# A mixture-of-experts block on one core: token rows scattered to memory in slot order, and blocks turned by VectorE

## What is computed

```python
h = _rmsnorm(x, pre_norm_w)                       # here x is xn
a = sigmoid(h @ w_a + decay_bias); i_gate = sigmoid(h @ w_i); v = h @ w_v
rec_out = _chunked_scan(a, sqrt(clip(1 - a*a, 1e-8)) * (i_gate * v))
x = x + rec_out @ out_proj_w
h2 = _rmsnorm(x, ffn_norm_w)
gate, up = split(h2 @ w_gate_up, 2)               # 256 -> 2 x 1024
branch_1 = x + silu(gate) * up @ w_down           # 1024 -> 256
...
top_vals, top_idx = top_k(xn @ w_router, 2)       # 8 experts, two per token
probs = softmax(top_vals)
branch_2 = sum over the two experts e of  probs_e * (square(relu(xn @ w_fc[e])) @ w_proj[e])
```

## Time and profile before

| | |
|---|---|
| median of 3 runs | 288.37 us (287.87 to 289.13) |
| the profiled execution's own time | 287.88 us |
| its span, first to last instruction | 286.1 us |

### The profile page before, as it was taken

One profiled execution on the slowest core, in us unless ns is written; L12 is line 12 of the kernel. 1 busy time (PEld: TensorE's weight loads), 2 busy tenths in 40 slices (PEclk: granted clock), 3 DMA queues, 4 the chain that ended last, 5 costly groups with the idle time before them and its releaser, 6 DMA issues.

```text
span 286.1 us, 5565 instructions
## 1 busy us (share of the span) xinstructions
PE 277.3 (97%) x1781; PEld 244.2 (85%) x1781; DVE 202.6 (71%) x467; ACT 171.2 (60%) x366; POOL 145.9 (51%) x139
## 2 busy tenths in 40 slices
PE   5989999999999999999999999999999999999995
PEld 5867778789889888898999789989999999887895
DVE  3899999999988888745557786545456544446973
ACT  3798889989669455536675554546568454532331
POOL 6498020433840136774878776666777775620000
PEclk9999999999999999999999999999999999999999
DMA  6999990018993002344345444434444445449922
GB/s 204 358 375 383 385 410 2 0 14 143 259 268 68 19 25 47 65 74 56 60 74 78 74 58 74 75 57 58 76 77 72 81 68 64 51 97 354 307 75 76
DMA packets 32584, 36.92 MB, mean 129 GB/s; under 512 B 4390, under 2 KB 29740, under 8 KB 32524
## 3 DMA queue, kind: packets, MB, share of 16 engines
q0 software_dynamic: 9616, 13.01, 28.4%
q1 hardware_dynamic: 20672, 21.31, 22.6%
q10 hardware_dynamic: 2268, 2.23, 2.2%
HBM read 24.68 MB, written 13.96 MB: 135 GB/s over the span
## 4 chain that ended last, share of the span: by engine, by line
PE 77%; DMA 9%; DVE 5%; issue 3%; POOL 3%; ACT 1%; POOLq 0%; SPq 0%; DVEq 0%; ACTq 0%
PE ps L401 63%; DMA acc_dram<-yb,gather_u 7%; PE ps L489 5%; PE ps L667 5%; DMA sums<-acc_dram 2%; PE ps L405 1%; PE ps L502 1%; PE ps L418 1%; DVE hT_lo L1103 1%; POOL rn L1522 1%; DVE Wpj_lo L1264 1%; DVE guT_lo L1274 0%; DVE stats L1075 0%; DVE X L1306 0%; DVE dec L1134 0%
## 5 line engine op out<-in xcount | busy, mean ns | idle before, releaser
L1570 POOL DMA_INDIRECT xg<-xh_dram,gather_u x39 | 46.5, 1192 | 47.3 <-DVE picks L1331 34.0
L1579 POOL DMA_INDIRECT acc_dram<-yb,gather_u x39 | 62.0, 1591 | 16.3 <-issue 9.2
L401 PE MATMUL ps<-h2T_lo,Wgu_hi 128*128 128x512 f32 (+1 forms) x132 | 42.9, 386 | 0.0
L401 PE MATMUL ps<-h2T_hi,Wgu_hi 128*128 128x512 f32 (+1 forms) x132 | 40.9, 391 | 0.0
L401 PE MATMUL ps<-h2T_hi,Wgu_lo 128*128 128x512 f32 (+1 forms) x132 | 40.1, 385 | 0.0
L401 PE MATMUL ps<-Wd_hi,guT_hi 128*128 128x256 f32 x128 | 36.3, 284 | 0.6 <-DVE guT_lo L1274 0.5
L1348 DVE TENSOR_TENSOR aT_lo<-ps,aT_hi 128x256 fp32r<-128x256 f32 x39 | 16.5, 424 | 28.1 <-ACT aT_hi L926 27.7
L401 PE MATMUL ps<-Wd_hi,guT_lo 128*128 128x256 f32 x128 | 36.2, 282 | 0.0
L401 PE MATMUL ps<-Wd_lo,guT_hi 128*128 128x256 f32 x128 | 36.1, 282 | 0.0
L884 ACT ACTIVATE gu<-ps 128x512 f32<-128x512 f32 x31 | 18.4, 595 | 20.4 <-PE ps L401 20.4
L1269 DVE TENSOR_TENSOR gu<-gu,ps 128x512 f32<-128x512 f32 x31 | 21.2, 684 | 13.0 <-PE ps L401 11.6
(11 more groups left out here) (194 smaller groups left out, 665.6 us busy)
## 6 DMA issues: line engine op xcount, KB each, us to landing
sums<-acc_dram SPq DMA_DIRECT2D x8, 512.0 KB, 7.5
acc_dram<-zero SPq DMA_DIRECT2D x1, 2176.0 KB, 14.6
Wgu_raw<-in_L_attn_w_gate_up_dram SPq DMA_DIRECT2D x4, 512.0 KB, 9.1
Wfc_raw<-in_L_ffn_w_fc_dram SPq DMA_DIRECT2D x4, 512.0 KB, 13.9
xh_dram<-X ACTq DMA_DIRECT2D x4, 512.0 KB, 7.7
Wpj_raw<-in_L_ffn_w_proj_dram SPq DMA_DIRECT2D x4, 512.0 KB, 9.8
X<-in_L_attn_x_dram SPq DMA_DIRECT2D x3, 512.0 KB, 6.7
out_dram<-X SPq DMA_DIRECT2D x3, 512.0 KB, 4.8
```

Source lines behind the costliest of these rows:

```text
L401: return nc.tensor.matmul(dst, lhs, rhs, start=start, stop=stop, skip_group_check=group)
L1570: pool.indirect_dma_start(out=xg[i % XG][:, :], out_offset=None, in_=xh_dram, in_offset=bass.IndirectOffsetOnAxis(ap=gather_u[:, i:i + 1], ...
L1579: pool.indirect_dma_start(out=acc_dram[i % 2], in_=yb[i % YB][:, :], in_offset=None, compute_op=ALU.add, out_offset=bass.IndirectOffsetOnA ...
```

## The change

The inversion of the slot list goes. Instead each token row, with its weight and its home (the row to which its output goes) in two more columns, is scattered by GpSimd to a DRAM array `xs_dram` in slot order: 32 indirect stores of 128 rows (16 groups of tokens, two experts each). The array is first filled with blank rows. SP then loads pairs of blocks from it, each in eight transfers of 32 columns on 32 partitions, so that 32x32 squares lie together; VectorE transposes the squares (`block_turn`), one block ahead, and TensorE no longer turns blocks. The weights and homes of all slots are loaded once (`of_slot`). An expert's output row is written, without addition, to its own row of `y_dram`, one of two for each token; SP loads both sets as the two sums. x itself is added to the residual by an accumulating transfer of GpSimd's (`add_x`). Weight pieces 6 to 10 are halved by ScalarE and VectorE, as the others, instead of by accumulating transfers. The blocks move from slices 8 to 23 to slices 9 to 24. The rows of x lie 258 instead of 256 numbers apart in SBUF.

The diff, cut to its core:

```diff
-        FIRST = 8
-        LAST = 23
-        THREE = (14, 19, 23)
+        FIRST = 9
+        LAST = 24
+        THREE = (14, 19, 24)
...
@@ the list of SP @@
+            sp.dma_start(xs_slot[:, :, 0:D], blank[:, None, :].to_broadcast([P, 2 * NP, D])).then_inc(blank_stored, 16)
+            sp.dma_start(xs_slot[:, :, D:ROW].bitcast(I32), no_home[:, :, :]).then_inc(blank_stored, 16)
...
-            sp.wait_ge(routed, 1)
             sp.wait_ge(experts_ready, 1)
             for n in range(UNDER_ROUTING, ALL):
                 load_piece(n)
+            for b in range(B):
+                sp.wait_ge(rows_stored[b], 16 * TOP * J)
+            for n in range(NP):
+                if n >= XQ:
+                    sp.wait_ge(turned, 2 * (n - XQ) + 2)
+                for r in range(P // Q):
+                    mine = xq[n % XQ][r * Q:(r + 1) * Q].rearrange("i v g k c -> i (v g) k c")
+                    for k in range(K):
+                        col = k * P + r * Q
+                        sp.dma_start(mine[:, :, k, :], xs_pair[n, :, :, col:col + Q]).then_inc(xq_loaded[n % XQ], 16)
+                if n == 0:
+                    sp.dma_start(of_slot[:, :, :], xs_slot[:, :, WEIGHT:ROW]).then_inc(of_slot_loaded, 16)
             sp.wait_ge(fc_done, NB)
...
@@ the list of PE @@
-                if d == SLOTS:
-                    slots()
...
             def expert_in(i):
-                if i < NB:
-                    pe.wait_ge(xg_loaded[i % XG], 16 * (i // XG + 1))
...
-                    block_transpose(T1, xg[i % XG], t1_done)
...
@@ the list of DVE @@
             def add_residual(b, side):
                 dve.wait_ge(q_ready, 1)
-                dve.wait_ge(xh_stored[b], 16)
+                if b:
+                    dve.wait_ge(rows_stored[b], 16 * TOP * J)
...
+            def block_turn(i):
+                if i < NB:
+                    dve.wait_ge(xq_loaded[i // 2 % XQ], 16 * K * (P // Q) * (i // 2 // XQ + 1))
+                    if i >= 2:
+                        dve.wait_ge(xg_hi, i - 1)
+                    V.transpose(xr[i % 2][:, :, :].rearrange("p k (g s) -> p k g s", s=Q),
+                                xq[i // 2 % XQ][:, i % 2, :, :, :].rearrange("p g k c -> p k g c")).then_inc(turned, 1)
...
             gated_value(2, 1)
-            blocks(0)
-            blocks(1)
             weights_lo(5)
             gated_value(3, 0)
-            lanes(0)
-            lanes(1)
+            gated_value(3, 1)
             up(0)
-            lanes(2)
-            gated_value(3, 1)
+            cumulate(1, 0)
             split_gu(0)
             up(1)
-            lanes(3)
+            recur(1, 0)
             split_gu(1)
...
+            weights_lo(9)
+            weights_lo(10)
+            up(6)
             weights_lo(11)
-            up(6)
+            split_gu(6)
+            split_h2(1)
             weights_lo(12)
-            split_gu(6)
+            up(7)
             weights_lo(13)
-            split_h2(1)
-            up(7)
+            split_gu(7)
             weights_lo(14)
+            up(8)
+            take_down(0, 0)
+            block_turn(0)
+            block_in(0)
             for d in range(FIRST, B * M):
                 if d <= LAST:
                     for v, i in enumerate(blocks_of(d)):
-                        block_in(i)
+                        block_turn(i + 1)
...
                         block_square(i)
-                        block_weight(i)
+                        block_in(i + 1)
                         if i == 0:
                             weights_lo(16)
...
@@ the list of POOL @@
+            def mark_rows(k, first, end):
+                if k == 0:
+                    pool.wait_ge(prob_ready, TOP)
+                else:
+                    for b in range(first, end):
+                        pool.wait_ge(rows_stored[b], 16 * J)
+                n = end - first
+                mine = slice(J * first, J * end)
+                for b in range(first, end):
+                    G.iota(home_col[:, b, :], pattern=[[P, J]], base=k * N + b * J * P, channel_multiplier=1)
+                chain.step(G.tensor_tensor(weight_col[:, first:end, :],
+                                           prob[:, k, mine].rearrange("p (b j) -> p b j", j=J),
+                                           q2[:, mine].rearrange("p (b j) -> p b j", j=J), ALU.mult))
+            def store_rows(k, b):
+                if k == 0 and b == 0:
+                    pool.wait_ge(slots_ready, 1)
+                    pool.wait_ge(blank_stored, 32)
+                for j in range(J):
+                    n = k * T + b * J + j
+                    pool.indirect_dma_start(out=xs_dram, in_=rows_x[:, b, j, :], in_offset=None,
+                                            out_offset=bass.IndirectOffsetOnAxis(ap=slot_u[:, n:n + 1], axis=0)
+                                            ).then_inc(rows_stored[b], 16)
+            def add_x(b):
+                pool.wait_ge(h2_ready, b + 1)
+                pool.dma_start(Y[b][:, :, :], x_t[b], accum_op=ALU.add).then_inc(x_added[b], 16)
...
             def scatter(i):
                 pool.wait_ge(y_ready, i + 1)
-                if i >= 2:
-                    pool.wait_ge(*added(i - 2))
-                pool.indirect_dma_start(out=acc_dram[i % 2], in_=yb[i % YB][:, :], in_offset=None, compute_op=ALU.add,
-                                        out_offset=bass.IndirectOffsetOnAxis(ap=gather_u[:, i:i + 1], axis=0)
-                                        ).then_inc(y_added[i % 2], 16)
+                if i == 0:
+                    pool.wait_ge(of_slot_loaded, 16)
+                pool.indirect_dma_start(out=y_dram, in_=yb[i % YB][:, :], in_offset=None,
+                                        out_offset=bass.IndirectOffsetOnAxis(ap=of_slot[:, i, 1:2].bitcast(U32), axis=0)
+                                        ).then_inc(y_stored[i % YB], 16)
...
             root_h2(0)
-            token_weights()
...
-            weights_whole(10)
+            mark_rows(0, 0, B)
+            for b in range(B):
+                store_rows(0, b)
+            mark_rows(1, 0, B - 1)
+            store_rows(1, 1)
+            add_x(0)
+            store_rows(1, 0)
+            store_rows(1, 2)
+            mark_rows(1, B - 1, B)
             root_h2(1)
+            store_rows(1, 3)
+            add_x(1)
```

More of the change, by code:

```diff
@@ L197, in recurrent_moe_block @@
         over = [moe_at]
-        xg = [small(f"xg{u}", [P, ROW]) for u in range(XG)]
+        xr = [small(f"xr{u}", [P, K, P]) for u in range(2)]
         xgT = [(small(f"xgT{u}_hi", [P, K, P], F32R), small(f"xgT{u}_lo", [P, K, P], F32R)) for u in range(2)]
@@ L202, in recurrent_moe_block @@
         yb = [small(f"yb{u}", [P, D]) for u in range(YB)]
-        assert over[0] <= moe_at + 20 * KB - 256
+        assert over[0] <= moe_at + 16 * KB
+        assert J * ROW >= XQ * 2 * D
+        xq = [put(f"xq{u}", [P, 2, P // Q, K, Q], F32, X_at + 2 * D * 4 * u) for u in range(XQ)]
         h2 = [h2_first] + [put("h2", [P, J, D], F32, cum_at)] * (B - 1)
@@ L1295, in take_down @@
                     dve.wait_ge(down_done, M * (b + 1))
-                two = X[b][:, 2 * side:2 * side + 2, :].rearrange("p j d -> p (j d)")
-                last = V.tensor_tensor(two, two, ps[:, DOWN + side, :], ALU.add)
+                if side == 0:
+                    dve.wait_ge(x_added[b], 16)
+                two = Y[b][:, 2 * side:2 * side + 2, :]
+                last = V.tensor_tensor(two, two, ps[:, DOWN + side, :].rearrange("p (j d) -> p j d", d=D), ALU.add)
                 if side == 1:
```

326 lines of the change are left out of this document (113 added, 213 removed).

## The result

The median after the change is 294.59 us (294.03 to 295.02, four runs) against 288.24 us of the kernel before beside it: a ratio of 1.0236, interval 1.0206 to 1.0265. The profiled execution took 294.48 us with a span of 292.7, again 1.8 outside the span. The forecast was 292.0, 1.3% slower, in a range of 281 to 300.

What follows compares the result with a forecast made beforehand. TensorE was taken to bound the kernel. Span 286.1 - 9.9 (removed work and late wait) + 9.7 (late first expert layer) + 3.8 (pile) = 289.7 us, as a median 292.0, 1.3% slower; range 281 to 300.

Steps and rivals of the forecast that it cites:

- The price of a store: GpSimd's list ahead of the blocks: a store takes 1.19 us plus 0.31 idle, 1.50, stretched by VectorE's two-operand work.
- the 1.7 taken off the 28: Stores ahead of batch 1's root: 1.7 us less, as some seven between 53 and 61 us cost 1.26 beside idle VectorE.
- Rival B: GpSimd's stores: each costs what an accumulating scatter does, 1.55 + 0.31 us; run 303.3 us; chance 0.14.
- The blank rows: SP's queue ahead of the first store: blank rows end near 33.5 us, before the slots are known at 46.5.
- The root at 92.6: GpSimd, behind 28 stores: the root of batch 1's second norm is ready at 92.6 us.
- The wait of 7.2 ahead of the transposes: TensorE ahead of batch 1's second-norm transposes: they come at 94.5 us instead of 87.3, a wait of 7.2.
- rival A: Stores not held up, 1.26 us each; VectorE's new order sets the time; run 284.7 us, faster; chance 0.30.
- The first expert layer at 107.5: TensorE's start of the blocks: block loads and VectorE's queue put it at 107.5 us, 9.7 late, the 7.2 included.
- The pile, 3.8: VectorE at block 0: 8.3 us of queued work ahead of the second layer's split, against TensorE's 4.5: 3.8 us waiting.
- The clock: TensorE's granted clock: 1.00 in both views of the kernel before, 2.4 GHz, so it plays no part.
- Rival C: Block stage: the eight loads of a pair only half overlap, 12 us a pair; run near 395 us; chance 0.03.
- Rival D: TensorE: the removed transposes and slot products were hidden, so the change frees nothing; no chance of its own.

Runs made afterwards that it cites:

- Experiment 4: Kernel after without the second round of stores, 16 instead of 32, both sums fetched from the first half of the outputs: 287.25 us, ratio 0.9973 to the kernel before.
- 1: Kernel after with GpSimd computing the root of batch 1's second norm eight stores earlier: 295.21 us, ratio 1.0256 to the kernel before.
- 6: Kernel after with the blocks two slices later, seven slices of three blocks, and batch 1's root eight stores earlier: 293.10 us, ratio 1.0187 to the kernel before.
- 3: Kernel after with VectorE's low halves computed by scalar-tensor-tensor instead of tensor-tensor subtraction, same values: 294.70 us, ratio 1.0242 to the kernel before.
- 11: Kernel after with VectorE's low weight halves made zero by a one-operand product instead of a two-operand subtraction: 287.50 us, ratio 0.9996 to the kernel before.
- experiment 2: Kernel after with TensorE filling its waits ahead of batch 1's transposes and the first second layer with small products: 293.40 us, ratio 1.0197 to the kernel before.
- experiment 12: Kernel after with blocks from slice 11, root earlier, blank rows earlier, x added later, VectorE, TensorE and load order rearranged: 281.97 us, ratio 0.9788 to the kernel before.
- experiment 5: Kernel after with blocks from slice 11 instead of 9, seven slices of three blocks, VectorE's block 0 work moved earlier: 296.33 us, ratio 1.0313 to the kernel before.

## Why the prediction was right, and where it was not

**Direction and cause: right.** TensorE bounds, the removed work came off (its last 10 us of fetching sums are full), and the store list in GpSimd's order, through the root and the loads, took it back. Experiment 4 shows the list, and 1 and 6 show that both its waiters bind.

**The price of a store: right.** A store takes 0.96 at the least, the gather's 0.947, with 0.30 between two. The mean is 1.151 + 0.30 = 1.45 against 1.50, or against 1.44 with the 1.7 taken off the 28. Rival B's 1.55 + 0.31 is out. The stretch, which the prediction read from one gather beside one VectorE operation, is real, and experiments 3 and 11 show its rule: the remainder of the operation that runs when the store starts. The Trainium skill's page SBUF — State Buffer (Who interferes with whom) has both halves: it infers that writing descriptors is not delayed by a two-input operation, and it states that such an operation does contend with a GpSimd instruction that reads SBUF. The rows fit the second at the store's start, and the first for the 0.83 us that follow; that a store reads SBUF at its start only is an inference, which no run here shows.

**The blank rows: wrong.** The step "the blank rows are no obstacle", ended near 33.5 from bytes and rates, failed. The rows themselves landed at 44.2 and their homes at 47.9, which is 1.8 us behind the slots; first stores stood between 46.7 and 50.8 in the runs. The homes came last: 5120 records of 8 bytes, only 40 KB, with 18.95 us of issue on SP and 33.3 to landing behind the rows. Bytes over a rate don't price such a transfer. How much of the rows' own 10.7 us of delay comes from the homes beside them isn't shown.

**The root at 92.6: right, by errors that cancel.** Measured 92.78. The list started 2.3 late; the two marking steps were 1.3 cheaper than the 2.4 they were priced at, the 28 stores 0.6 and the root 0.35.

**The wait of 7.2 ahead of the transposes: 4.52.** They stood at 94.57, predicted 94.5; TensorE came there at 90.05 instead of 87.3, and 2.3 of that are VectorE's new order (0.97 and 1.36, measured above). That was put under rival A alone; it was there in either case, under cover.

**The first expert layer at 107.5: 108.59.** The loads set it, as said, but by 0.1 us alone; SP's eight issues took 4.7 us instead of 3.6.

**The pile, 3.8: 2.48** in waiting, with the queue that was named. The twelve operations took 7.5 us from 108.37 instead of 8.3, for operations in a row overlap by about 0.1 each. TensorE had 5.0 us of work in that time instead of 4.5; the pieces named for the 4.5 add up to 4.2. The 1.6 us of low clock stand behind the wait.

**The clock: a step that failed.** That the clock "plays no part", since it was granted in full in the kernel before, was read off a kernel without long waits, and the change made three. Of the two losses, 2.1 and 1.6, only the second is in the time (experiment 2). The first filled most of the gap of 2.5 that was foreseen ahead of the first expert layer, where 1.01 was found.

**The sum.** The span was 292.7, not 289.7. First expert layer +1.1, pile -1.3, clock +1.6, small waits in the blocks +0.8 (1.6, of which the kernel before had 0.8): 2.2 of the 3.0. Another 0.35 stands behind TensorE's last product (3.43 us instead of 3.08). Where the rest went was not found.

**Rival A** decides at a store below 1.35 with its gap, and it was 1.45. Its own number was good: with half of the stores gone, VectorE's order sets the first expert layer at 102.0, as its 97.8 + 4.3 says. **Rival C**: the 160 loads are covered, TensorE has 19.84 of 20 us between 140 and 160. **Rival D** is out: the removed work counts in experiment 12.

## What to carry to other kernels

Where work is taken off the bounding engine by putting a list of transfers ahead of a stage, write down who waits for the list's end and what work can stand in front of them: here 32 stores ahead of the blocks cost 2.4% with one slice of cover, and with three slices, the root moved up and the order mended, the change gave 2.1%. More cover alone was slower still (experiment 5). Lift all the waiters together, for one lifted alone hands its wait to the next (experiments 1 and 2) or leaves the other in place (5). And price a wait of the bounding engine with what its clock does behind it.

## What the runs showed of the hardware

- An indirect store of 128 rows takes 0.96 us, and 0.30 stand between two. If its start falls into a VectorE operation with two SBUF operands (or a one-operand one of 0.69 us for 1024 columns), it ends about 0.83 us behind that operation; beside one with an operand in PSUM it takes 0.96 to 1.04 (experiments 3 and 11). The first store of a list takes some 0.26 more, and one that starts 0.04 behind the start of a scan isn't held (1.22 at 48.82 and 0.96 at 70.17 in the kernel after).
- 5120 records of 8 bytes took 18.95 us to issue and 33.3 to land, behind 5 MB in the same queue; read back in one transfer, 5.2 to landing.
- Behind the waits of 4.52 and 2.48 us of the kernel after, TensorE's granted clock was at the lower level (0.50 from 94.57 to 98.90, 0.54 on the mean from 116.09 to 119.82). Behind 1.86 us it was so in experiment 6, but not in 11, nor behind 2.18 there. With small products in the first two waits it stayed at 1.00 (experiment 2).
